# A local-attention transformer on one core: the score mask in the scores' own array tiling, norm turns on the full array, and new step orders on five engines

## The chip, the cores and the metric

One core of a Trainium2 chip. The metric is the device time of one launch in microseconds. TensorE multiplies (its records are PE, its weight loads PEld), VectorE is DVE, ScalarE is ACT, GpSimd is POOL, SyncE is SP, which here only issues DMAs.

## What is computed

A first stage (layer norm, one attention without softmax, gates) is run once for each of 16 batches of 256 tokens with 128 channels. Then six layers, each for all 16 batches, of local attention with 16 heads of 64 and windows of 32 tokens, and of a gated feed-forward net. The change is in the attention:

```python
q = l2norm(q) * qs;  k = l2norm(k) * ksc            # norms over each head's 64 channels
q = q*cos*scale + rotate_half(q)*sin*scale           # k with 1/scale
bk2, bv2 = look(bk), look(bv)                        # the window before and this one: 64 keys
mask = (it < jb) | (it > jb + w) | (jb == -1)
sim = jnp.where(mask, -finfo.max, einsum('bhwie,bhwje->bhwij', bq, bk2) * 8.0)
out = einsum('bhwij,bhwje->bhwie', softmax(sim, -1), bv2)
```

`it` is the place of the query, `jb` of the key (-1 ahead of the first window), `w` is 32. All of it is float32.

## The kernel before

Channels lie on the partitions and tokens in the free dimension. One *period* of the main part does one batch's share of everything, and 96 batches (6 layers x 16) pass through it in three stages. `walk(order, step)` goes through an engine's order once per period; a step is done for batch g of that period, for g + 1 if its kind is in `AHEAD`, for g - 1 if it is in `BEHIND`. The orders are strings written out by hand at the top (`PE_ORDER`, `DVE_ORDER`, `ACT_ORDER`, `POOL_ORDER`, `SP_ORDER`). Engines are tied only by semaphores: `x.wait_ge(sem, at(g, n, k))` waits for k of the n events that batch g brings.

The steps of TensorE, in the trace by their lines:
- PA, PB 0 to 3 (L1234, ahead): projections of k (0, 1) and q (2, 3), halves a and b of each head.
- V0 to V3 (L1279, ahead): values. 
- NK, NQ (L1245, ahead): sums of squares of k and q per head, with `head_ones` loaded in four column tiles of 32; TK, TQ (L1253): their transposes.
- TU (L1260, ahead): turns `rk_bf`, the inverse norms of k in three bf16 parts, 3 x 16 = 48 columns, so that heads lie on partitions. UC copies it to `rkt`. KN0, KN1 (L1269, ahead) spread it over the channels with `head_sel_bf`, 48 rows deep.
- S00, S01, S10, S11: scores of token tile 0 and 1, in two halves of 64 matmuls each. Each matmul is 64 rows by 32 columns of the array (`qt` loaded, `kt` moving, 64 columns): 2 banks (e) by 4 windows (w) is 8 places. Ahead of S00 and S10 the mask is put into the two banks (L1289): identity times `mask_bf`, 128x128, 512 columns.
- T (L1308): transposes of the probabilities; PV (L1326): probabilities times values, 64x64 pieces.
- WO (L1336), CEN, VAR (L1350, L1354), UP (L1365), DN (L1372), BI (L1345), all behind: output projection, layer norm, feed-forward.

DVE: XS copies the shifted input, RA and RB (L993) multiply the projections with the rotary tables, M (L1026, L1031) takes row maxima, XA and XB (L1059 to L1064) add the residual behind WO, AR (L1045) inverts the sums, KM (L1009) scales k, TC (L1038), UC and VC (L1015) copy out of PSUM. ACT: Q squares (L730), E exponentials (L774), OC (L763) and VC (L736) copies, RTK and RTQ norms, G gelu. POOL: AD0 to AD3 (L617) add the two products into `ks` (0, 1) and `qs` (2, 3), AN (L601) divides the probabilities, RK (L587 to L595) splits the inverse norms into bf16 parts, TB0 to TB3 (b = 15 of a layer only) make the next layer's tables.

SP issues, in its order, only once the wait in front of each is over:
- MQ and MK (L476): `move`, 8 DMAs of 128 KB each, from `qs` to `qt` and from `ks` to `kt`. MQ waits for AD3 (`rot_ready`), MK for KM1 (`kn_ready`); both are of the batch ahead, and S00 of the next period waits for them.
- MV (L487): `move_v`, 16 DMAs from `vs` to `v2`, after the period's last PV and the VC copies.
- LS, LK, LV, LL: loads of the next layer's weights. LK and LV only for b = 15 of their batch, LL for b = 4, layers 0 to 4. LV (L454, 512 KB) first waits for the last V of its batch, as `wv` has one buffer. LL (L458 to L466) is five loads, 1 MB.

PSUM: the steps PA, PB, TU, KN, V, T, DN (and PAD, a place left empty) take three banks in turn, `ring_ps`; a step waits until the reader of the step three places before is done (`bank_free`).

Of the kernel before, what the change touches and what calls it, by code (L numbers as in the profile page):

```python
# [8 lines left out]
BF16 = mybir.dt.bfloat16  # L9
# [4 lines left out]
P = 128  # L14
BATCH, TOKENS, DIM = 16, 256, 128
DEPTH, HEADS, DIM_HEAD, WINDOW = 6, 16, 64, 32
# [3 lines left out]
PAIRS = HEADS // 2  # L20
TILES = TOKENS // P
WINDOWS = TOKENS // WINDOW
WPT = P // WINDOW
KEYS = 2 * WINDOW
# [3 lines left out]
HALF = DIM_HEAD // 2  # L28
QUADS = HEADS // 4
COUPLES = QUADS // 2  # L30
QK_BANKS = 4 * COUPLES
MOVES = 8
V_MOVES = 16
# [5 lines left out]
MASKED = -1e30  # L39
# [11 lines left out]
PA0 PB0 PA1 S00 S01 PB1 BI WO PA2 NK CEN PB2 VAR PA3 PB3 TK UP0 UP1 S10 S11 V0 UP2 T00 TU NQ KN0 PAD V1 PV00 KN1  # L51
TQ T01 V2 DN T10 PV01 V3 T11 PV10 PV11
"""
DVE_ORDER = """
XS RA0 RB0 RA1 M0 RB1 BI XA XB AR00 RA2 RB2 CK XG RB3 RA3 H0 M1 AR01 H1 TC00 UC H2 KM0 CQ VC1 KM1 AR10 TC01 X
AR11 TC10 VC3 TC11
"""
ACT_ORDER = """
QA0 QB0 QA1 E00 QB1 E01 E02 SQ QA2 LN E03 QB2 RTK LG G0 QB3 QA3 G1 VC0 G2 LE E10 E11 E12 E13 VC2 OC00 OC01 OC10
RTQ OC11  # L60
"""
POOL_ORDER = """
AD0 AD1 AD2 AN00 AD3 RK TB0 AN01 TB1 AN10 TB2 AN11 TB3
"""
SP_ORDER = """
LS LK MQ MK LV LL MV
# [52 lines left out]
def build(nc, t):  # L119

    with ExitStack() as ctx:
        def sb(name, shape, dt=F32):
            return ctx.enter_context(nc.sbuf_tensor(name, shape, dt))
# [5 lines left out]
        score_ps = [ctx.enter_context(nc.psum_tensor(f"score_ps{e}", [P, 512], F32)) for e in range(2)]  # L129
# [9 lines left out]
        mask_bf = sb("mask_bf", [P, TILES, PAIRS, KEYS], BF16)  # L139
        head_ones = sb("head_ones", [P, WINDOW])  # L140
        head_sel_bf = sb("head_sel_bf", [3 * HEADS, QUADS, P], BF16)
# [32 lines left out]
        rk_bf = sb("rk_bf", [P, TILES, 3, HEADS], BF16)  # L174
        rkt = sb("rkt", [3 * HEADS, TOKENS], BF16)
# [105 lines left out]
        mask = carve(P, TILES, KEYS)  # L281
        head_sel = carve(3 * HEADS, QUADS, P)
# [58 lines left out]

        def moved(g, n=0, moves=MOVES):

            return (g + n) * (16 * moves)
# [57 lines left out]
        def bank_of(s):  # L402

            return ring_ps[RING.index(s) % BANKS]
# [14 lines left out]
        def _(sp):  # L419
# [20 lines left out]
            for dst, src in ((mask[:, :, :], t["mask"]), (head_ones[:, :], t["head_ones"]),  # L440
                             (head_sel[:, :, :], t["head_sel"]), (rotary[:, :, :], t["rotary"])):
                sp.dma_start(dst, src).then_inc(consts_landed, 16)
# [90 lines left out]
        def _(pool):  # L533
# [4 lines left out]
            pool.memset(ones_bf[:, :], 1.0)  # L538
            pool.memset(kt[:, :, 0:WINDOW], 0.0).then_inc(memset_done, 1)
# [7 lines left out]
            pool.wait_ge(consts_landed, 16 * 4)  # L547
# [5 lines left out]
            for i in range(TILES):  # L553
                for j in range(PAIRS):
                    last = pool.tensor_copy(mask_bf[:, i, j, :], mask[:, i, :])
# [255 lines left out]
        def _(dve):  # L811
# [161 lines left out]
            def step(s, g, b, parity, layer):  # L973
# [24 lines left out]
                if kind == "UC":  # L998
                    dve.wait_ge(rk_turned, at(g, 1, 1))
                    dve.wait_ge(kn_made, at(g, COUPLES))  # L1000
                    turn = bank_of(("TU",))[0:3 * HEADS, 0:TOKENS // 2].bitcast(BF16)
                    V.tensor_copy(rkt[:, :], turn).then_inc(rkt_ready, 1)
                if kind == "KM":
                    c = s[1]
# [88 lines left out]
        def _(pe):  # L1093
# [129 lines left out]
            def step(s, g, b, parity, layer):  # L1223
# [31 lines left out]
                if kind == "TU":  # L1255
                    pe.wait_ge(rk_parts, at(g, 4, 4))
                    bank_free(g, s)
                    turn = bank_of(s)[0:3 * HEADS, 0:TOKENS // 2].bitcast(BF16)
                    for i in range(TILES):
                        last = pe.transpose(turn[:, P * i:P * (i + 1)],  # L1260
                                            rk_bf[:, i, :, :].rearrange("p a h -> p (a h)"), ident_bf[:, :])
                    last.then_inc(rk_turned, 1)
# [18 lines left out]
                if kind == "S":  # L1281

                    i, half = s[1], s[2]
                    if half == 0:
                        pe.wait_ge(exp_ready, at(g, TILES * PARTS, PARTS * i))
                        for e in range(2):
                            if e == 1 and i == 0:
                                pe.wait_ge(q_moved, moved(g, 1))
                            mm(score_ps[e][:, :], ident_bf[:, :], mask_bf[:, i, :, :].rearrange("p j c -> p (j c)"),  # L1289
                               start=True, stop=False, skip_group_check=True)  # L1290
# [98 lines left out]
def shape_constants():  # L1389
# [12 lines left out]
    query = np.arange(P)[:, None] % WINDOW  # L1402
    key = np.arange(KEYS)[None, :]
    hidden = (key > query + WINDOW) | (query > key)
    mask = np.zeros((P, TILES, KEYS), np.float32)
    for i in range(TILES):
        no_window = (i == 0) & (np.arange(P)[:, None] < WINDOW) & (key < WINDOW)
        mask[:, i] = np.where(hidden | no_window, MASKED, 0.0)
    head_ones = np.zeros((P, WINDOW), np.float32)
    head_sel = np.zeros((HEADS, QUADS, P), np.float32)  # L1410
    for r in range(4):
        head_ones[HALF * r:HALF * (r + 1), r] = 1.0
        for u in range(QUADS):
            head_sel[4 * u + r, u, HALF * r:HALF * (r + 1)] = 1.0
    return {"ident": np.eye(P, dtype=np.float32), "mask": mask, "head_ones": head_ones,
            "head_sel": np.concatenate([head_sel] * 3), "rotary": rotary,
# [40 lines left out]
```

## Time and profile before

| what | us |
|---|---|
| median of 3 runs (lowest, highest) | 3449.61 (3441.67, 3456.11) |
| the profiled execution, its own time | 3448.65 |
| its span, first to last instruction | 3446.9 |
| busy: PE, ACT, DVE, POOL | 3333.7, 2701.8, 2439.3, 1445.0 |
| mean granted clock of TensorE | 0.991 |

The first scores start at 197.7 us; what is before them is the first stage. In the rows, start and duration stand ahead of the engine; starts count from the span's start. Every float32 matmul leaves two records, as it goes through the array in parts. The end of a matmul in the rows is modelled, so the time that a group takes is best read from its start to the next group's start.

### The profile page before, as it was taken

The page shows a single profiled execution, that of the slowest core. Times are in us where ns is not written, and L with a number is a line of the kernel's source. Part 1 is how long each engine was busy: PE and PEld are TensorE (multiplying, and loading weights), DVE is VectorE, ACT ScalarE, POOL GpSimd, SP SyncE. Part 2 cuts the span into 40 slices and gives each one's busy share as a digit, 9 for nine tenths or more (in the row PEclk, how much of TensorE's full clock was granted, in tenths as well). Part 3 has the DMA queues.
Part 4 walks back from the last instruction along what each step waited for, and adds up shares of the span by engine and source line. Part 5 has one row for each costly group of instructions (what it writes and reads, how often), then busy time and mean ns, then how long its engine had stood idle before and what let it go on. Part 6 is the DMA issues. An engine that isn't in the chain of part 4 may idle for free.

```text
span 3446.9 us, 152524 instructions
## 1 busy us (share of the span) xinstructions
PE 3333.7 (97%) x63228; PEld 2469.4 (72%) x63228; DVE 2439.3 (71%) x5141; ACT 2701.8 (78%) x9033; POOL 1445.0 (42%) x1276
## 2 busy tenths in 40 slices
PE   7789999999999999999999999999999999999997
PEld 4457777777777777777777777777777777777775
DVE  5667777777777777777777777777777767777773
ACT  5667887878787787878788787877878787887875
POOL 2244443444444354444444443453434444443441
PEclk9999999999999999999999999999999999999998
DMA  2056655665655666565565655565565656556563
GB/s 73 1 109 132 131 123 126 134 136 115 147 118 125 129 137 132 128 131 123 120 148 117 139 128 128 122 138 127 121 141 120 132 127 133 122 121 136 114 135 75
DMA packets 361274, 421.43 MB, mean 122 GB/s; under 512 B 52291, under 2 KB 265814, under 8 KB 359814
## 3 DMA queue, kind: packets, MB, share of 16 engines
q1 hardware_dynamic: 360582, 411.67, 55.2%
q8 instruction: 499, 8.18, 1.0%
q14 instruction: 193, 1.58, 0.1%
HBM read 19.30 MB, written 2.10 MB: 6 GB/s over the span
## 4 chain that ended last, share of the span: by engine, by line
PE 70%; POOL 18%; issue 4%; DVE 2%; ACT 1%; DMA 0%; SPq 0%; POOLq 0%; DVEq 0%
PE ring_ps L1234 16%; POOL qs L617 13%; PE out_ps L1326 12%; PE out_ps L1336 10%; PE ring_ps L1279 8%; PE small_ps L1245 6%; PE score_ps L1297 4%; PE ring_ps L1308 4%; PE ring_ps L1372 4%; POOL probs L601 3%; DVE prod L993 2%; PE ring_ps L1269 2%; PE out_ps L1350 2%; PE score_ps L1289 1%; PE small_ps L1253 1%
## 5 line engine op out<-in xcount | busy, mean ns | idle before, releaser
L774 ACT ACTIVATE probs<-score_ps,neg_max,rq 128x64 f32<-128x64 f32 x3072 | 1194.7, 420 | 95.7 <-DVE neg_max L1031 94.5
L993 DVE TENSOR_TENSOR prod<-ring_ps,tables 128x512 f32<-128x512 f32 x1536 | 956.9, 680 | 285.6 <-PE ring_ps L1234 257.8
L617 POOL TENSOR_TENSOR ks<-prod 128x1024 f32<-128x1024 f32 x192 | 452.7, 2358 | 852.5 <-DVE prod L993 852.4
L1234 PE MATMUL ring_ps<-xs,wqk 128*128 128x256 f32 x3072 | 768.9, 388 | 15.5 <-issue 10.6
L774 ACT ACTIVATION_READ_ACCUMULATOR probs<-score_ps,neg_max,rq 128x1 f32 x3072 | 677.1, 220 | 0.0
L730 ACT ACTIVATE square<-ring_ps,biases 128x512 f32<-128x512 f32 x768 | 516.9, 687 | 197.2 <-DVE prod L993 196.0
L1234 PEld LDWEIGHTS ring_ps<-xs,wqk 128*128 128x128 f32 x3072 | 571.1, 191 | 104.3 <-issue 17.6
L601 POOL TENSOR_TENSOR probs<-probs,inv_sums 128x512 f32<-128x512 f32 x384 | 401.1, 1045 | 576.0 <-DVE inv_sums L1045 576.0
L617 POOL TENSOR_TENSOR qs<-prod 128x1024 f32<-128x1024 f32 x192 | 453.4, 2361 | 395.4 <-DVE prod L993 395.4
L1326 PEld LDWEIGHTS out_ps<-pt,v 64*64 64x64 f32 x24576 | 397.0, 135 | 113.5 <-issue 111.6
L763 ACT ACTIVATE att_t<-out_ps 128x512 f32<-128x512 f32 x384 | 217.0, 591 | 297.3 <-PE out_ps L1326 297.2
L1326 PE MATMUL out_ps<-pt,v 64*64 64x32 f32 x24576 | 430.2, 221 | 6.9 <-issue 4.8
L1279 PE MATMUL ring_ps<-wv,xs 128*128 128x512 f32 x768 | 425.5, 636 | 0.7 <-ACT vs L736 0.7
L1336 PE MATMUL out_ps<-att_t,wo 128*128 128x256 f32 x1536 | 351.6, 382 | 2.2 <-ACT att_t L763 1.2
L1297 PEld LDWEIGHTS score_ps<-kt,qt 64*32 64x32 f32 x24576 | 264.4, 105 | 90.6 <-issue 82.2
L1336 PEld LDWEIGHTS out_ps<-att_t,wo 128*128 128x128 f32 x1536 | 293.2, 191 | 43.4 <-issue 1.8
L1038 DVE COPY pt<-ring_ps 128x512 f32<-128x512 f32 x384 | 259.3, 675 | 82.0 <-PE out_ps L1326 78.5
L1297 PE MATMUL score_ps<-kt,qt 64*32 64x64 f32 x24576 | 297.6, 225 | 6.4 <-issue 4.0
L1009 DVE TENSOR_TENSOR ks<-ks,ring_ps 128x512 f32<-128x512 f32 x384 | 246.6, 683 | 64.3 <-PE ring_ps L1269 63.9
L1365 PE MATMUL out_ps<-xg,w 128*128 128x256 f32 (+1 forms) x1152 | 282.3, 381 | 3.5 <-DVE xg L1069 3.2
L1026 DVE TENSOR_REDUCE row_max<-score_ps 128x8 f32<-128x512 f32 x384 | 246.2, 683 | 22.8 <-PE score_ps L1297 18.9
L1365 PEld LDWEIGHTS out_ps<-xg,w 128*128 128x128 f32 (+1 forms) x1152 | 198.1, 179 | 80.7 <-DVE hidden L1076 30.9
(182 smaller groups left out, 3835.6 us busy)
## 6 DMA issues: line engine op xcount, KB each, us to landing
v<-vs SPq DMA_DIRECT2D x1344, 128.0 KB
qt<-qs SPq DMA_DIRECT2D x768, 128.0 KB
kt<-ks SPq DMA_DIRECT2D x768, 128.0 KB
v<-vs SPq DMA_DIRECT2D x192, 64.0 KB
wqk<-in_L_ffn_Wqkv SPq DMA_DIRECT2D x6, 1024.0 KB, 5.1
wv<-in_L_ffn_Wqkv SPq DMA_DIRECT2D x6, 512.0 KB, 5.8
wo<-in_L_ffn_Wo SPq DMA_DIRECT2D x6, 512.0 KB
out_dram<-ks SPq DMA_DIRECT2D x16, 128.0 KB, 1.9
```

Source lines behind the costliest of these rows:

```text
L601: pool.tensor_tensor(probs[i][:, part, :, :].rearrange("p j e k -> p (j e) k"), probs[i][:, part, :, :].rearrange("p j e k -> p (j e) k"), ...
L617: pool.tensor_tensor(dst, prod_a[p % 2], prod_b[p % 2], ALU.add).then_inc(rot_ready, 1)
L730: nc.scalar.activation(square[p % COUPLES][a][:, :], bank_of(("PB" if a else "PA", p))[:, :], ACT.Square, bias=zero_col[:, :]).then_inc(sq ...
L774: last = nc.scalar.activation(probs[i][:, j, e, :], score_ps[e][:, KEYS * j:KEYS * (j + 1)], ACT.Exp, bias=neg_max[:, h:h + 1], scale=rq[p ...
L993: last = V.tensor_tensor((prod_b if a else prod_a)[p % 2][:, f, :] .rearrange("p (u c) -> p u c", u=2), bank[:, :].rearrange("p (u c) -> p ...
L1038: V.tensor_copy(pt[:, 4 * c:4 * c + 4, :], bank_of(("T", i, c))[:, :].rearrange("p (j c) -> p j c", c=P)).then_inc(t_copied, 1)
L1234: last = mm(bank_of(s)[:, TOKENS * f:TOKENS * (f + 1)], wqk[:, n, 2 * c + f, a, :], xs[:, WINDOW:PADDED], start=True, stop=True)
L1279: mm(bank_of(s)[:, :], xs[:, WINDOW + P * i:WINDOW + P * (i + 1)], heads[:, :, e, :], start=True, stop=True).then_inc(v_made, 1)
L1297: last = mm(score_ps[e][WINDOW * w:WINDOW * (w + 1), KEYS * j:KEYS * (j + 1)], qt[64 * e:64 * e + 64, j, q0:q0 + WINDOW], kt[64 * e:64 * e ...
L1326: last = mm(out_ps[j % 2][side:side + 64, q0:q0 + WINDOW], v2[64 * e:64 * e + 64, WPT * i + w, DIM_HEAD * j:DIM_HEAD * (j + 1)], pt[64 * e ...
L1336: last = mm(out_ps[0][:, 0:TOKENS], wo[layer % 2][:, j, :], att_t[:, j, :], start=(j == 0), stop=(j == PAIRS - 1))
L1365: last = mm(out_ps[c % 2][0:size, TOKENS * n:TOKENS * (n + 1)], w1[layer % 2][:, col:col + size], xg[:, :], start=True, stop=True)
```

## The change

1. The mask. Before: per token tile two matmuls of 128x128 with 512 columns. After: eight of 64x32 with 512 columns, one for each of the eight places that the scores use; `mask_sel_bf` (identity of 32, and a row that switches the first window's extra mask on) is loaded and the 64-row `mask_bf` moves. q's moves are waited for ahead of the last of the eight; it was ahead of the second of two.
2. Norm turns on the full array. `rk_bf` gets 8 parts instead of 3 (five stay zero), so TU is 128x128 instead of 128x48 and KN 128x128 instead of 48x128; UC copies 128 rows.
3. The orders of all five engines. Among other things: S00 and S01 come right behind PA0 (before: behind PA0, PB0 and PA1); TU comes ahead of T01 and behind V1; KN0 and KN1 stand together behind PV00; POOL does AN00 ahead of AD1, and RK and AN01 ahead of AD3; TB0 to TB3 stand at the end; ACT's VC2 comes behind OC10; on SP, LV and LL stand ahead of MK, which was ahead of both.

```diff
 PE_ORDER = """
-PA0 PB0 PA1 S00 S01 PB1 BI WO PA2 NK CEN PB2 VAR PA3 PB3 TK UP0 UP1 S10 S11 V0 UP2 T00 TU NQ KN0 PAD V1 PV00 KN1
-TQ T01 V2 DN T10 PV01 V3 T11 PV10 PV11
+PA0 S00 S01 BI PB0 PB1 PA1 WO PA2 PB2 NK CEN PA3 TK VAR S10 S11 PB3 UP0 T00 UP1 UP2 V1 TU T01 PAD NQ PV00 KN0
+KN1 DN PV01 V0 V3 T10 TQ V2 T11 PV10 PV11
 """
 DVE_ORDER = """
-XS RA0 RB0 RA1 M0 RB1 BI XA XB AR00 RA2 RB2 CK XG RB3 RA3 H0 M1 AR01 H1 TC00 UC H2 KM0 CQ VC1 KM1 AR10 TC01 X
-AR11 TC10 VC3 TC11
+XS RA0 BI M0 RB0 RA1 RB1 XA XB AR00 RB2 CK RA2 RA3 XG AR01 RB3 H0 TC00 M1 H1 H2 VC1 TC01 UC KM0 KM1 AR10 CQ X
+AR11 VC3 TC10 TC11
 """
 ACT_ORDER = """
-QA0 QB0 QA1 E00 QB1 E01 E02 SQ QA2 LN E03 QB2 RTK LG G0 QB3 QA3 G1 VC0 G2 LE E10 E11 E12 E13 VC2 OC00 OC01 OC10
-RTQ OC11
+QA0 E00 QB0 E01 QB1 QA1 E02 E03 SQ QB2 QA2 LN RTK LG G0 QA3 QB3 G1 G2 LE E10 E11 E12 E13 VC0 OC00 OC01 OC10 VC2
+OC11 RTQ
 """
 POOL_ORDER = """
-AD0 AD1 AD2 AN00 AD3 RK TB0 AN01 TB1 AN10 TB2 AN11 TB3
+AD0 AN00 AD1 AD2 RK AN01 AD3 AN10 AN11 TB0 TB1 TB2 TB3
 """
 SP_ORDER = """
-LS LK MQ MK LV LL MV
+LS LK MQ LV LL MK MV
 """
...
-        rk_bf = sb("rk_bf", [P, TILES, 3, HEADS], BF16)
-        rkt = sb("rkt", [3 * HEADS, TOKENS], BF16)
+        rk_bf = sb("rk_bf", [P, TILES, RK_PARTS, HEADS], BF16)
+        rkt = sb("rkt", [P, TOKENS], BF16)
...
             pool.memset(ones_bf[:, :], 1.0)
+            pool.memset(rk_bf[:, :, :, :], 0.0)
...
-            for i in range(TILES):
-                for j in range(PAIRS):
-                    last = pool.tensor_copy(mask_bf[:, i, j, :], mask[:, i, :])
+            pool.tensor_copy(mask_sel_bf[:, :, :], mask_sel[:, :, :])
+            for j in range(PAIRS):
+                last = pool.tensor_copy(mask_bf[:, j, :], mask[:, :])
...
-                    turn = bank_of(s)[0:3 * HEADS, 0:TOKENS // 2].bitcast(BF16)
+                    turn = bank_of(s)[:, 0:TOKENS // 2].bitcast(BF16)
...
-                        for e in range(2):
-                            if e == 1 and i == 0:
-                                pe.wait_ge(q_moved, moved(g, 1))
-                            mm(score_ps[e][:, :], ident_bf[:, :], mask_bf[:, i, :, :].rearrange("p j c -> p (j c)"),
-                               start=True, stop=False, skip_group_check=True)
+                        for w in range(WPT):
+                            for e in range(2):
+                                if (w, e) == (WPT - 1, 1) and i == 0:
+                                    pe.wait_ge(q_moved, moved(g, 1))
+                                mm(score_ps[e][WINDOW * w:WINDOW * (w + 1), :],
+                                   mask_sel_bf[64 * e:64 * e + 64, int((i, w) == (0, 0)), :],
+                                   mask_bf[64 * e:64 * e + 64, :, :].rearrange("p j c -> p (j c)"),
+                                   start=True, stop=False, skip_group_check=True)
                     if i == 0 and half == 0:
                         pe.wait_ge(k_moved, moved(g, 1))
```

## Rows read from the trace of the kernel before

**Rows 1.** Stretch view, first to last output projection: length, busy times, granted clock, DMA share, GB/s

```profile
236.40:3416.60 3180.20, 3140.70 (x61776) 2343.76 (x61775) 2287.16 (x4629) 2554.66 (x8533) 1380.22 (x1171) 1.00 0.59 128
```

**Rows 2.** Timeline of TensorE, one period: start us, duration us, engine, line, operation, out<-in

```profile
1708.01 0.59 PE L1289 MATMUL score_ps<-mask_bf,ident_bf 128*128 128x512 bf16 x2
1708.53 1.64 PE L1297 MATMUL score_ps<-kt,qt 64*32 64x64 f32 x128
1710.10 1.13 PE L1234 MATMUL ring_ps<-xs,wqk 128*128 128x256 f32 x4
1711.07 3.62 PE L1336 MATMUL out_ps<-att_t,wo 128*128 128x256 f32 x16
1714.52 1.03 PE L1234 MATMUL ring_ps<-xs,wqk 128*128 128x256 f32 x4
...
1725.74 0.60 PE L1308 MATMUL ring_ps<-ident,probs 128*128 128x128 f32 x4
1726.40 0.29 PE L1260 MATMUL ring_ps<-ident_bf,rk_bf 128*48 128x128 bf16 x2
1726.62 1.07 PE L1245 MATMUL small_ps<-square,head_ones 128*32 128x256 f32 x16
1727.62 0.39 PE L1269 MATMUL ring_ps<-rkt,head_sel_bf 48*128 48x256 bf16 x2
1727.94 1.12 PE L1279 MATMUL ring_ps<-wv,xs 128*128 128x512 f32 x2
1729.00 1.14 PE L1326 MATMUL out_ps<-pt,v 64*64 64x32 f32 x64
1730.07 0.39 PE L1269 MATMUL ring_ps<-rkt,head_sel_bf 48*128 48x256 bf16 x2
1730.39 0.44 PE L1253 MATMUL small_ps<-ident,norm 128*128 128x128 f32 x2
...
1741.64 1.75 PE L1297 MATMUL score_ps<-kt,qt 64*32 64x64 f32 x128
```

**Rows 3.** Timelines of DVE (first row) and POOL in the same period

```profile
1715.95 0.19 DVE L1045 RECIPROCAL inv_sums<-sums 128x8 f32<-128x8 f32 x1
...
1722.80 2.36 POOL L617 TENSOR_TENSOR qs<-prod 128x1024 f32<-128x1024 f32 x1
1726.30 1.04 POOL L601 TENSOR_TENSOR probs<-probs,inv_sums 128x512 f32<-128x512 f32 x1
```

**Rows 4.** Timeline of SP's queue: issues of q's and k's moves, two periods

```profile
385.09 6.54 SPq L476 DMA_DIRECT2D qt<-qs  x8
...
1725.25 5.33 SPq L476 DMA_DIRECT2D qt<-qs  x8
1731.87 5.50 SPq L476 DMA_DIRECT2D kt<-ks  x8
```

**Rows 5.** Stretch view around these moves, columns as in rows 1

```profile
391.74:392.90 1.16, 1.16 (x7) 1.01 (x7) 0.54 (x1) 1.16 (x8) 1.04 (x1) 1.00 0.98 195
...
1733.00:1738.90 5.90, 5.90 (x206) 4.83 (x206) 3.15 (x7) 2.94 (x10) 1.06 (x2) 1.00 0.88 183
1738.90:1739.70 0.80, 0.80 (x6) 0.70 (x5) 0.11 (x1) 0.77 (x4) 0.00 (x0) 1.00 0.00 0
```

**Rows 6.** Timeline of SP's queue where a layer's weights are loaded

```profile
364.38 0.59 SPq L458 DMA_DIRECT2D wo<-in_L_ffn_Wo  x1
...
368.55 0.61 SPq L487 DMA_DIRECT2D v<-vs  x1
...
1235.19 0.59 SPq L454 DMA_DIRECT2D wv<-in_L_ffn_Wqkv  x1
```

**Rows 7.** Stretch view around a stall of TensorE, columns as in rows 1

```profile
765.04:766.73 1.69, 0.00 (x1) 0.00 (x0) 0.00 (x0) 0.00 (x0) 0.00 (x0) 1.00 0.05 10
766.73:770.60 3.87, 3.87 (x12) 3.12 (x12) 1.29 (x2) 1.96 (x5) 0.00 (x0) 0.56 0.35 77
```

## What I expect, and why

> **What bounds the kernel now.** I read four views in this order. First the busy time of the whole repeating part [rows 1]: from the first output projection to the last, 3180.2 us for 95 periods, 33.48 us each, and TensorE is busy for 3140.7 of them. So TensorE sets the time, and the question is what fills it. Second its timeline in one period [rows 2]. It repeats after 33.11 us (scores at 1708.53 and 1741.64) and runs without a hole. A step of four full-array records takes 0.86 us (WO: 16 in 3.45). Where the array's tiling changes there is more: PB1, right behind the scores, takes 0.97; V1, between the 48-row KN0 and the 64x64 PV00, takes 1.06. So a group pays 0.10 when it follows a change of tiling and 0.10 when one follows it. Third POOL and DVE around the q and k rotations [rows 3], and last the SP queue's moves and the DMA engines' share [rows 4, 5], because the new order puts the scores much nearer to the moves that feed them. In what follows times are counted from the start of the first score matmul of a period, "score 0".
>
> **Full-array norm turns.** T00 to KN1 take 4.65 us now (1725.74 to 1730.39) [rows 2]: T00 0.66, TU 0.22, NQ 1.00, KN0 0.32, V1 1.06, PV00 1.07, KN1 0.32. T00 carries 0.12 in which TU waits for POOL's rk_bf (RK ends as AN starts, 1726.30 [rows 3]). With TU and KN full and the new order, the same work is T00 0.43, TU 0.11, V1 0.86 with 0.10 before NQ, NQ 1.00, PV00 1.07, KN0 0.32 (first after a change), KN1 0.21, together 4.10. Saving 0.55 per period. The 128 rows instead of 48 cost nothing, since time goes by columns: KN still has 256. RK moves ahead of AN01 and AD3 on POOL, so TU no longer waits.
>
> **The mask.** Now two bf16 matmuls of 512 columns per token tile, 0.52 us with 0.10 for the change before the scores [rows 2]: 0.42, or 0.21 each. After: eight of 64x32, each on its own piece of the array, in the scores' own tiling. Bounds: all eight together, 0.21; one after another, 8 x 0.21 = 1.7. Nearest row: NQ, 16 records of 256 columns and two passes in four column tiles, takes 1.00 us, from 1726.62 to 1727.62 [rows 2], where one after another would be 16 x 0.216 = 3.45. The four tiles overlap almost fully. The scores say the same for the rows: 128 records of 64 columns take 1.57, or 12 ns each, where one alone would be 54 (0.216 x 64/256). I take 0.25 and keep both ends. Saving 0.17 twice, 0.35 per period. The change of tiling itself isn't saved, it now lies before the mask.
>
> The Trainium skill (TensorE: Matmul & The Clock Gate, Part 3) gives 10.6 times for 16 tiles of 512 columns, a little worse than I take; an estimate by it is 8 x 0.21 / (8 x 0.66) = 0.32 per mask, 13 us more over the kernel.
>
> TensorE's own work falls by 0.9, from 33.1 to 32.2 us per period. If it stayed the bound, 95 x 0.9 = 86 us would go.
>
> **The new order, against what the moves need.** Score 0 of a batch needs all 16 moves of its q and k (MQ, MK; 1 MB each), which DVE's KM1 and POOL's AD3 of the period before release. Now PA0, PB0 and PA1 stand ahead of score 0; after, only PA0. MK is issued at 1731.87 and score 0 comes at 1741.64, 9.77 us later [rows 2, 4]. Its packets end at 1738.9, 7.0 after the issue [rows 5]; that is a good case. In another period MQ is issued at 385.09 [rows 4] and the engines are still at share 0.98 from 391.74 to 392.90 [rows 5], 7.8 after it, so a set takes 7.0 to some 8.5, and score 0 has had 1.3 to 2.8 us of room.
>
> After, on POOL: WO ends at 7.7 (scores 1.57, PB0 0.97, PB1 and PA1 1.72, WO 3.45). XA, XB and AR00 follow it as now, until 1.6 later (1714.52 to 1716.14) [rows 2, 3]: 9.3. AN00 now comes ahead of AD1: 10.4. AD1 and AD2 at 2.36 each: 15.2. RK 1.2: 16.4. AN01 1.04: 17.4. AD3: 19.8 [rows 3]. Nothing of this leaves POOL idle. RB3, which AD3 also needs, is done by 16.9. MQ is issued from 19.9 (now 16.7), its eight issues take 5.2, and KM1 is done at 24.8; so MK starts at 25.1, right behind MQ instead of 1.3 us after its last issue, and lands 7.0 to 8.7 later, plus up to 0.5 since MQ's packets are still in the engines. I take 8.0: 33.1, with 0.1 for the semaphore 33.2. TensorE would be there at 32.2. So it waits about 1 us at every score 0, and the period is 33.2 (bounds 32.2 and 34.0), hardly below today's 33.11.
>
> Part of today's mean over 33.11 (0.37) lies in short stalls of TensorE before the scores, such as the 1.69 us from 765.04 [rows 7]; behind a wait for DMA most of it is covered. I take 33.25 as the mean: 95 x (33.25 - 33.48) = -22 us.
>
> The Trainium skill (DMA: Bandwidth & Descriptors, Specifications) lets packets of 512 B and more run at up to 435 GB/s. An estimate by it has the moves limited by their issues alone, and the wait gone. The rows show 183 GB/s at share 0.88 with 1 KB packets [rows 5], so the trace disagrees.
>
> **What is queued ahead of MK on SP.** The new SP order has LV and LL before MK; both are there five times (layers 0 to 4). LL issues five loads and holds SP for 4.2 us (364.38 to 368.55) [rows 6]; now only the v moves stand behind it. MK starts at 29.3 instead of 25.1 and the wait for it grows by 4.1. LV first waits for V2. PV10 and PV11 (2.1), T11 (0.5), PA0 (0.96) and the mask (0.25) lie between V2's end and the next score 0, so V2 ends near 28.3; LV's issue is 0.6 [rows 6]: MK starts at 29.0, and half a megabyte of weights shares the engines with it (2.9 us at 180 GB/s; I take half): 5.5. Together 5 x 9.6 = 48 us. Bounds: 3 and 7 for each, 30 to 70.
>
> With waits of 5 to 6 us the clock comes in. After 1.69 us of idle the granted clock was 0.56 for 3.87 us [rows 7], most of it at the lower of its two levels, 1.2 GHz: 3.87 x 0.44 = 1.7 us lost. I price each of the ten long waits with that: 17 us (0 to 35).
>
> LL's data is wanted much later, and TB0 to TB3 now stand behind AN11: DVE's first rotation of a layer comes 1.4 us later, under LV's wait. VC2 now comes behind OC10 and delays the v moves by 1.3 us, with 7 to spare before PV00. The smaller mask set-up lies under the first stage. All at nothing; without LV's wait TB would cost 5 x 1.4 = 7 us.
>
> **Sum.** 3448.65 (the profiled execution's time; span 3446.9, median of the runs 3449.61) - 22 + 48 + 17 = 3492; I say 3490.
>
> **Rivals.**
> - *The moves land in time*: 12.3 us after MQ's issue (5.2 + 7.1, as in the good case). The wait vanishes and the mean is 32.2 + 0.37 = 32.6: -84, + 65 at the layers' ends: 3430. For it: the good case is real. Against: MQ's packets in front. 0.18.
> - *Moves in time and the layers' ends nearly free* (SP gets through LL and LV under other work): 3365. Against: there is nothing between MK and score 0 that could wait. 0.07.
> - *The transfers of a pair queue up fully* (slower side, one mechanism): both sets at 7 us of packets, 1.2 + 14, give a period of 34.1; from 13.6 us for the pair on the kernel is slower even without the layers' ends. 95 x 0.6 + 65: 3570. 0.12.
> - *The eight mask matmuls don't overlap* (the change doesn't do what it says): 1.7 instead of 0.42. The first lies partly in the wait, the second adds 1.3 per period: 3610. NQ's row speaks against it. 0.04.
> - *Forecast*, 3455 to 3535: 0.55. 0.04 for what lies between it and the first rival.
>
> The range is 3400 to 3560, leaving out most of the second, third and fourth rival. A measurement of this kernel can tell 0.5% from no change: faster than 3432, 0.22 (second rival, most of the first); between, 0.18; slower than 3467, 0.60.
>
> **What would show it.** In the profile after: T00 to KN1 near 4.1 us; each mask group about 0.25 ahead of the scores; TensorE waiting for DMA kt at nearly every score 0, about 1 us, and ten times 5 us or more, with the clock down behind them; SP's MK issue 5.2 us after MQ's, and 9 us after it ten times. If score 0 waits for nothing in ordinary periods, the first rival holds. If the period is under 32.5 my walk of POOL or the transfer time is wrong.

## The result and the profile after

After takes 3656.44 us in the median (3642.6 to 3671.03), before 3451.07 beside it: a ratio of 1.0599 [1.0552, 1.0646], 205 us slower. The forecast was 3490 in a range of 3400 to 3560. The sign was right, the size was not. The profiled execution of after took 3655.21 us, with a span of 3653.4 and a mean granted clock of 0.963; before it was 3446.9 and 0.991. Times here and below are medians of fast executions; the one slow execution, 3744.09 us at a granted clock of 0.844, of the second kernel of experiment 3, is left out.

The busy time of the repeating part comes first, first to last output projection (length, busy times, granted clock, DMA share, GB/s), after:

```profile
241.08:3623.27 3382.19, 3127.98 (x62907) 2382.20 (x62906) 2322.01 (x4629) 2530.09 (x8526) 1376.38 (x1172) 0.97 0.53 120
```

A period is now 35.60 us instead of 33.48 [rows 1]. TensorE is busy for 12.7 us less in all, although its clock is lower. It stands idle for 254 us where it was idle for 40: 215 more, less the 12.7, are the 202 us by which this part grew. The waits of TensorE (line waited for, sum, times, longest), after and then before:

```profile
PE score_ps L1304 <- DMA kt<-ks: 193.0, 81, 6.2
PE out_ps L1333 <- issue: 27.2, 16, 2.1
...
PE score_ps L1304 <- issue: 20.4, 25, 1.9
```

```profile
PE ring_ps L1234 <- issue: 10.6, 13, 1.6
...
PE score_ps L1297 <- issue: 4.0, 5, 1.7
...
PE score_ps L1297 <- DMA kt<-ks: 2.3, 3, 1.6
```

There are 96 batches, and score 0 waits for k's moves 81 times; before, 3 times. The chain that ended last says the same: SP's issues (23%) and POOL (21%) are on it nearly as much as TensorE is (29%).

```profile
PE 29%; SPq 23%; POOL 21%; issue 12%; DMA 7%; DVE 3%; ACT 0%; POOLq 0%; DVEq 0%
```

One period on TensorE's timeline, after, answers [rows 2]:

```profile
1730.59 0.41 PE L1294 MATMUL score_ps<-mask_bf,mask_sel_bf 64*32 64x512 bf16 x8
1730.82 1.40 PE L1304 MATMUL score_ps<-kt,qt 64*32 64x64 f32 x113
1733.14 0.34 PE L1304 MATMUL score_ps<-kt,qt 64*32 64x64 f32 x15 [0.93 <-issue]
1733.41 2.86 PE L1238 MATMUL ring_ps<-xs,wqk 128*128 128x256 f32 x12
1736.11 3.62 PE L1343 MATMUL out_ps<-att_t,wo 128*128 128x256 f32 x16
...
1751.01 0.27 PE L1264 MATMUL ring_ps<-ident_bf,rk_bf 128*128 128x128 bf16 x2
1751.12 0.61 PE L1315 MATMUL ring_ps<-ident,probs 128*128 128x128 f32 x4
...
1763.62 0.41 PE L1294 MATMUL score_ps<-mask_bf,mask_sel_bf 64*32 64x512 bf16 x8
1767.71 1.69 PE L1304 MATMUL score_ps<-kt,qt 64*32 64x64 f32 x128 [3.67 <-DMA kt<-ks]
1769.33 4.39 PE L1238 MATMUL ring_ps<-xs,wqk 128*128 128x256 f32 x12
```

TensorE's own work from score 0 to the end of the next mask is 1763.85 - 1730.82 - 0.93 = 32.1 us. The mask takes 0.23, TU 0.11 (1751.01 to 1751.12). Score 0 then waits until 1767.71, so this period is 36.89. And the twelve matmuls behind the wait take 4.39 instead of 2.86. The moves of the same two periods on SP's queue, against [rows 4]:

```profile
1716.42 5.91 SPq L479 DMA_DIRECT2D qt<-qs  x8
1722.45 6.40 SPq L479 DMA_DIRECT2D kt<-ks  x8
1730.88 10.76 SPq L490 DMA_DIRECT2D v<-vs  x16
1751.55 7.72 SPq L479 DMA_DIRECT2D qt<-qs  x8
1759.38 6.45 SPq L479 DMA_DIRECT2D kt<-ks  x8
```

MQ is issued 20.73 after score 0 (I had 19.9), its eight issues take 7.72 (I had 5.2), and score 0 comes 8.33 behind MK (I had 8.1). The stretches around that wait, columns as in the first row:

```profile
1763.98:1767.71 3.73, 0.06 (x9) 0.00 (x1) 1.04 (x2) 1.48 (x4) 0.00 (x0) 1.00 0.62 135
1767.71:1769.30 1.59, 1.59 (x128) 1.45 (x128) 0.00 (x0) 0.00 (x0) 0.00 (x0) 0.93 0.87 193
1769.33:1771.30 1.97, 1.97 (x7) 1.61 (x6) 1.47 (x3) 0.33 (x2) 0.00 (x0) 0.50 0.89 205
1771.30:1773.56 2.26, 2.26 (x9) 1.87 (x8) 1.29 (x2) 2.12 (x10) 0.75 (x1) 0.74 0.48 111
```

After 3.7 us with almost nothing on TensorE, the granted clock is 0.93 over the scores, and 0.50, the lower level of 1.2 GHz, for the first 2 us of the full-array work behind them.

The shown period is one of the longer ones. Over the 95 steps from one score 0 to the next in the trace of after, the median is 35.5 us and the mean 35.7; before, 33.2 and 33.5. In the ten periods with LV or LL the mean is 38.15, in the other 85 it is 35.4 and the median 35.3. In the median of these 85, MQ is issued 20.8 us after score 0, its issues take 6.0, MK starts 27.1 after score 0 and score 0 comes 8.2 behind MK.

**Where 206 us of span come from.** Waits for kt: 193.0 - 2.3 = 191. Waits called "issue" at the scores, the PV products and the projections: 20.4 + 27.2 + 8.0 against 4.0 + 4.8 + 10.6, 36. Slower matmuls in two groups whose work did not change, from the groups by line (busy time, mean ns), after and before:

```profile
L1238 PE MATMUL ring_ps<-xs,wqk 128*128 128x256 f32 x3072 | 829.5, 410 | 17.7 <-issue 8.0 <-ACT square L734 5.9 <-DVE xs L984 3.6
L1304 PE MATMUL score_ps<-kt,qt 64*32 64x64 f32 x24576 | 316.9, 241 | 213.6 <-DMA kt<-ks 193.0 <-issue 20.4
```

```profile
L1234 PE MATMUL ring_ps<-xs,wqk 128*128 128x256 f32 x3072 | 768.9, 388 | 15.5 <-issue 10.6 <-DVE xs L980 4.1 <-ACT square L730 0.7
L1297 PE MATMUL score_ps<-kt,qt 64*32 64x64 f32 x24576 | 297.6, 225 | 6.4 <-issue 4.0 <-DMA kt<-ks 2.3
```

That is 60.6 + 19.3 = 80. Less work: 95 x 0.9 = 86 the other way. The 86 is the forecast's saving. Sum: 191 + 36 + 80 - 86 = 221, within 15 of the 206; the ends of matmuls are modelled, so the 80 is the roughest. The slower matmuls gave back almost all of the saving, as the 12.7 us of busy time says too.

### The profile page after: what moved, and what is told of

Read it like the earlier page. It is cut to its first block, busy times and chain, and to the rows that moved or that the text cites. A ratio compares the mean times of both kernels' runs of the same rounds, so it can differ in the third digit from the quotient of the medians.

```text
span 3653.4 us, 154823 instructions
## 1 busy us (share of the span) xinstructions
PE 3318.9 (91%) x64380; PEld 2509.2 (69%) x64380; DVE 2472.5 (68%) x5141; ACT 2677.1 (73%) x9033; POOL 1437.7 (39%) x1270
## 3 DMA queue, kind: packets, MB, share of 16 engines
q8 instruction: 508, 8.32, 1.0%
## 4 chain that ended last, share of the span: by engine, by line
PE 29%; SPq 23%; POOL 21%; issue 12%; DMA 7%; DVE 3%; ACT 0%; POOLq 0%; DVEq 0%
SPq L479 23%; POOL qs L621 8%; POOL ks L621 8%; PE ring_ps L1238 8%; DMA kt<-ks 7%; PE score_ps L1304 6%; POOL probs L605 4%; PE out_ps L1343 3%; PE out_ps L1333 2%; PE ring_ps L1283 2%; PE out_ps L1372 2%; DVE prod L997 2%; PE small_ps L1249 1%; PE ring_ps L1315 1%; DVE row_max L1030 1%
## 5 line engine op out<-in xcount | busy, mean ns | idle before, releaser
L997 DVE TENSOR_TENSOR prod<-ring_ps,tables 128x512 f32<-128x512 f32 x1536 | 978.8, 685 | 433.9 <-PE ring_ps L1238 368.7
L1238 PE MATMUL ring_ps<-xs,wqk 128*128 128x256 f32 x3072 | 829.5, 410 | 17.7 <-issue 8.0
L778 ACT ACTIVATION_READ_ACCUMULATOR probs<-score_ps,neg_max,rq 128x1 f32 x3072 | 689.9, 225 | 0.0
L1238 PEld LDWEIGHTS ring_ps<-xs,wqk 128*128 128x128 f32 x3072 | 598.9, 203 | 126.4 <-issue 21.9
L734 ACT ACTIVATE square<-ring_ps,biases 128x512 f32<-128x512 f32 x768 | 506.5, 686 | 118.1 <-DVE prod L997 114.3
L1304 PE MATMUL score_ps<-kt,qt 64*32 64x64 f32 x24576 | 316.9, 241 | 213.6 <-DMA kt<-ks 193.0
L1304 PEld LDWEIGHTS score_ps<-kt,qt 64*32 64x32 f32 x24576 | 292.7, 112 | 250.2 <-DMA kt<-ks 218.5
L1333 PE MATMUL out_ps<-pt,v 64*64 64x32 f32 x24576 | 422.9, 220 | 28.5 <-issue 27.2
L767 ACT ACTIVATE att_t<-out_ps 128x512 f32<-128x512 f32 x384 | 226.6, 639 | 303.0 <-PE out_ps L1333 303.0
L1283 PE MATMUL ring_ps<-wv,xs 128*128 128x512 f32 x768 | 387.5, 606 | 1.7 <-DVE ks L1013 1.2
L1315 PEld LDWEIGHTS ring_ps<-ident,probs 128*128 128x128 f32 x1536 | 184.2, 141 | 114.7 <-POOL probs L605 72.9
```

The costliest lines, as they stand in the source:

```text
L734: nc.scalar.activation(square[p % COUPLES][a][:, :], bank_of(("PB" if a else "PA", p))[:, :], ACT.Square, bias=zero_col[:, :]).then_inc(sq ...
L778: last = nc.scalar.activation(probs[i][:, j, e, :], score_ps[e][:, KEYS * j:KEYS * (j + 1)], ACT.Exp, bias=neg_max[:, h:h + 1], scale=rq[p ...
L997: last = V.tensor_tensor((prod_b if a else prod_a)[p % 2][:, f, :] .rearrange("p (u c) -> p u c", u=2), bank[:, :].rearrange("p (u c) -> p ...
L1238: last = mm(bank_of(s)[:, TOKENS * f:TOKENS * (f + 1)], wqk[:, n, 2 * c + f, a, :], xs[:, WINDOW:PADDED], start=True, stop=True)
L1283: mm(bank_of(s)[:, :], xs[:, WINDOW + P * i:WINDOW + P * (i + 1)], heads[:, :, e, :], start=True, stop=True).then_inc(v_made, 1)
L1304: last = mm(score_ps[e][WINDOW * w:WINDOW * (w + 1), KEYS * j:KEYS * (j + 1)], qt[64 * e:64 * e + 64, j, q0:q0 + WINDOW], kt[64 * e:64 * e ...
```

## The experiments

The theory to begin with: the loss is the wait for the moves, with what it does to the clock. The rival: TensorE would be slow in the new order even with q and k in place.

**1. The wait taken away, the moves left.** The kernel after:

```diff
-                                if (w, e) == (WPT - 1, 1) and i == 0:
-                                    pe.wait_ge(q_moved, moved(g, 1))
...
-                    if i == 0 and half == 0:
-                        pe.wait_ge(k_moved, moved(g, 1))
...
-                                          qt[64 * e:64 * e + 64, j, q0:q0 + WINDOW],
-                                          kt[64 * e:64 * e + 64, j, q0:q0 + KEYS],
+                                          still_q[64 * e:64 * e + 64, j, q0:q0 + WINDOW],
+                                          still_k[64 * e:64 * e + 64, j, q0:q0 + KEYS],
```

> The changed kernel, but its score matmuls read a part of x1_all that doesn't change in the main part instead of qt and kt, and TensorE waits for no move ahead of the scores. The moves are still issued in full. So the scores are of other data; all work and all orders stay. Theory (the wait for the moves of k, and what follows from it, is the whole loss): TensorE runs at its own 32.0 us per period plus the short stalls of before, about 32.5, so 95 x 3.1 = 295 us less than 3655: 3360 (3340 to 3390), and the granted clock is back at 0.99. Rival (the new orders or the eight small mask matmuls let the clock fall or make TensorE stall by themselves, the moves are a bystander): 3550 or more, the clock near 0.96.

Measured 3472.64. This kernel, its counterpart below, and the two others whose scores are of unchanging data were executed once each. The same edit on the kernel before:

> The same edit on the kernel before: scores of unchanging data, no wait for moves ahead of them. Theory: the moves cost the kernel before next to nothing (4 us of waits in its rows), so 3435 to 3450. Rival (the moves held it up too, by contention or by short waits that no row shows): below 3420.

Measured 3451.46, as before without it: there the moves cost nothing. After loses 184 us with its wait. But the time is neither the theory's nor the rival's: without any wait for moves the new order still takes 3473 and not 3360, more than the kernel before. What holds TensorE there is new:

```profile
PE score_ps L1303 <- issue: 81.4, 88, 2.6
PE ring_ps L1241 <- issue: 22.9, 16, 2.7
```

In 88 places TensorE stands in the middle of the scores with no semaphore, buffer or transfer to wait for, as in this period:

```profile
1714.77 0.78 PE L1303 MATMUL score_ps<-x_all 64*32 64x64 f32 x52
1716.02 1.11 PE L1303 MATMUL score_ps<-x_all 64*32 64x64 f32 x76 [0.46 <-issue]
```

It runs out of instructions. PV10, PV11, PA0, the mask and S00 and S01 now follow each other: 128 + 4 + 8 + 128 records of matmuls, each with one of a weight load, some 540 instructions in about 4.7 us. (Float32 leaves two records for each matmul of the program, so S00 is 32 matmuls and 64 records.) Before, PB0 and PA1 stood in this stretch as well, and the mask was 2 matmuls and not 8.

The trace shows the fetches themselves, as packets of 16 KB on a DMA queue of kind "instruction". In the period shown such a packet ran from 1713.57 to 1714.62, and the scores went on at 1716.02, 1.40 after its end. That is the rule: from the first scores on, 122 of the 124 stalls of TensorE without a releaser end 1.1 to 1.7 us after the end of such a packet, where instants at random would do so in 9% of cases. In after it is 52 of 52, in before 29 of 29.

**2. The moves taken away too.** All q and k moves, and POOL's waits for them, are left out of the kernel of experiment 1.

> a_still without any move of q and k: MQ and MK still wait but issue nothing, and POOL's AD0 and AD2 don't wait for them. Tells apart two reasons for the missing instructions in S00. If the fetches (16 KB each) queue behind the moves' packets on the DMA engines, they come in time now: 3400 or less. If the stretch is simply denser than the fetches can follow, nothing changes: 3460 to 3480. I lean to the first, 60 to 40.

Measured 3412.1, 60 us less than 3472.64, and between the two expectations. The wait inside the scores falls from 81.4 to 49.8 us:

```profile
PE score_ps L1301 <- issue: 49.8, 65, 2.5
```

So part of it comes only with the moves, and the larger part stays without them. This kernel also shows the saving of the change where no move disturbs it: a period less TensorE's waits is 32.3 us in the mean, against 33.2 before.

**3. Full-array work between the small matmuls.** Two kernels: that of experiment 1, and after itself, with PB0 and PB1 ahead of the scores.

```diff
-PA0 S00 S01 BI PB0 PB1 PA1 WO PA2 PB2 NK CEN PA3 TK VAR S10 S11 PB3 UP0 T00 UP1 UP2 V1 TU T01 PAD NQ PV00 KN0
+PA0 PB0 PB1 S00 S01 BI PA1 WO PA2 PB2 NK CEN PA3 TK VAR S10 S11 PB3 UP0 T00 UP1 UP2 V1 TU T01 PAD NQ PV00 KN0
```

> a_still (scores of unchanging data, no wait for moves) with one edit in TensorE's order: PA0 PB0 PB1 S00 S01 BI PA1 instead of PA0 S00 S01 BI PB0 PB1 PA1, so that 1.7 us of work with 16 instructions more stands between the dense PV10, PV11 and the dense mask and scores. Theory (in a_still TensorE runs out of instructions in S00, 1.0 us in a median period, since PV10, PV11, PA0, mask and scores are some 540 instructions in 4.7 us): S00 and S01 back to 1.5 us, period 32.2 with the short stalls, 3400 (3370 to 3420), clock 0.99. Rival (the stall in S00 has another cause that goes with the scores wherever they stand): 3460 to 3480.

Measured 3545.53, far from both. The feeding theory holds in its own row, the wait inside the scores is back to 17.6 us. But the time rises by 73 us, since the other engines kept the order made for the old place of the scores:

```profile
PE ring_ps L1241 <- ACT square L737: 70.6, 95, 2.8
...
PE out_ps L1360 <- ACT xc_sq L789: 21.3, 95, 3.0
...
PE score_ps L1303 <- issue: 17.6, 21, 1.9
```

> The changed kernel with only TensorE's order PA0 PB0 PB1 S00 S01 BI PA1. The scores come 1.7 us later behind PV11 than in the changed kernel. Theory (the short way from the moves to the scores costs the time): most of the mean wait of 2.1 us goes, and with it the clock's 0.5 us and the missing instructions; M0 and all behind it come 1.7 us later, of which I expect some 0.3 us to show: 95 x 2.2 = 210 less, 3450 (3420 to 3500). Rival (the loop only turns later by as much, since AD3 and KM1 follow the scores): 3620 or more.

Measured 3581.03, 1.0383 [1.0362, 1.0405], 75 us better than after instead of 206. The moves have their room, 33.0 us of waiting in 28 batches instead of 193.0 in 81, and the same two waits for ACT stand in their place:

```profile
PE ring_ps L1238 <- ACT square L734: 68.9, 97, 2.3
PE score_ps L1304 <- DMA kt<-ks: 33.0, 28, 4.0
...
PE score_ps L1304 <- issue: 13.1, 18, 1.4
```

**4. The wait filled, with small matmuls or with full-array ones.** If the idle time lowers the clock and that costs time, then needless work in it should help.

```diff
-                        for w in range(WPT):
+                        for n, w in [(n, w) for n in range(10 if i == 0 else 1) for w in range(WPT)]:
```

> The changed kernel with the eight mask matmuls of token tile 0 done ten times over instead of once (the same result each time, 1.9 us more of TensorE's work, most of it in what is otherwise the wait for k's moves). Theory (the wait itself is paid by the moves, and on top of it the clock falls after it and makes PB0 to PA1 slower by 0.5 us in the mean, inside the loop that leads to the next moves): the clock stays up and the time falls by some 45 us in spite of more work, 3610 (3590 to 3640). Rival (the clock costs nothing, as the wait absorbs it): 3655 to 3700.

Measured 3761.7, 1.0898 [1.0882, 1.0914]: 105 us more than after, beyond the rival's own number; what it shows is the supply of instructions, not the clock. The wait for kt falls by 141 us and the wait for instructions rises by 65, which with 95 x 2.0 = 190 us of added masks makes 114:

```profile
PE score_ps L1304 <- issue: 85.4, 65, 2.5
PE score_ps L1304 <- DMA kt<-ks: 51.6, 36, 4.7
```

The page of the profile counts the fetches: 508 packets and 8.32 MB on the queue of kind "instruction" in after, 562 and 9.21 in this kernel. The 6912 added mask matmuls with their weight loads are 13,824 instructions, so one packet of 16 KB brings 256 of them. 508 packets are 130,048 instructions, and TensorE's matmuls and weight loads are 128,760 records, so nearly every record is an instruction of its own and these packets are TensorE's.

The same place filled with nine bf16 matmuls on the full array, 1.9 us and 18 instructions:

```diff
+                        for n in range(9 if i == 0 else 0):
+                            mm(score_ps[n % 2][:, :], ident_bf[:, :], mask_bf[:, :, :].rearrange("p j c -> p (j c)"),
+                               start=True, stop=True, skip_group_check=True)
```

> The clock's question again with few instructions, since a_fill took 144 more into a stretch that is short of them. The changed kernel with nine full-array bf16 matmuls of 512 columns (18 instructions, 1.9 us) between PA0 and the mask of token tile 0, into the two score banks, which the mask then overwrites; the result stays. Theory (after a wait for k's moves the clock falls and makes the loop to the next moves longer): the wait is filled, the clock is 0.98 or more, PB0 to PA1 are back at 2.7 us, and the time falls by 40 to 60 us, 3605. Rival (the clock doesn't matter): 3655 to 3690, as some waits are shorter than the filling.

Measured 3618.1, 1.051 [1.0488, 1.0532]: 38 us less than after, with 1.9 us of useless work in every period. The wait for kt is 42.7 us in 35 batches, the mean clock 0.988 instead of 0.963, and the projections' matmuls are nearly as fast as before:

```profile
L1238 PE MATMUL ring_ps<-xs,wqk 128*128 128x256 f32 x3072 | 785.8, 394 | 17.8 <-issue 8.4 <-ACT square L734 5.6 <-DVE xs L984 3.6
```

An idle wait is thus dearer than the same wait filled. It slows the twelve matmuls behind it, DVE and POOL get their q and k later, and the next moves start later: MQ is issued 20.8 us after score 0 in the median of after's 85 ordinary periods, 19.7 here.

**5. SP's order.** After with MK ahead of LV and LL, as before.

```diff
-LS LK MQ LV LL MK MV
+LS LK MQ MK LV LL MV
```

> The changed kernel with the SP order of before: LS LK MQ MK LV LL MV. Theory: only the ten periods at the layers' loads gain, 3.8 us each above an ordinary period in the trace after, so 38 us less: 3615 (3600 to 3630). Rival (the SP order is the main cause): below 3560. Rival (loads behind MK disturb the transfers as much as ahead of it): no change, 3650.

Measured 3616.18, 1.0476 [1.0444, 1.0509]: 40 us less than after, the wait for kt 156.4 instead of 193.0. The clock hardly moves, 0.968 from 0.963. One LL in after shows the mechanism:

```profile
362.58 5.91 SPq L479 DMA_DIRECT2D qt<-qs  x8
368.54 0.60 SPq L461 DMA_DIRECT2D wo<-in_L_ffn_Wo  x1
...
371.23 6.12 SPq L479 DMA_DIRECT2D kt<-ks  x8
```

MK starts 8.65 after MQ instead of 6.0, and score 0 waits 4.25 us there. That the expected 38 us came out is in part luck: they were worked out with 3.8 us for each of the ten periods, and the trace of after has 2.7 (38.15 against 35.4), which makes 27.

**6. AD3 ahead of AN01 on POOL**, so that MQ is released 1.04 us earlier.

```diff
-AD0 AN00 AD1 AD2 RK AN01 AD3 AN10 AN11 TB0 TB1 TB2 TB3
+AD0 AN00 AD1 AD2 RK AD3 AN01 AN10 AN11 TB0 TB1 TB2 TB3
```

> The changed kernel with POOL's AD3 ahead of AN01 (AD0 AN00 AD1 AD2 RK AD3 AN01). MQ is released 1.04 us earlier and with it, since MK queues behind MQ, the pair; AN01 ends as late as AD3 did and TensorE's T01 may wait some 0.3 us. Theory (the pair of moves released by AD3 closes the loop): about 0.9 us per period, 85 us less: 3570 (3550 to 3610). Rival (KM1's release of MK closes it): no more than 20 us.

Measured 3645.93, 1.0585 [1.0559, 1.0612]: 10 us, as the rival said, and the trace has its mechanism. In after MK is issued right behind MQ's last issue, 1.2 us after KM1's end (medians). Here MQ comes 0.75 us earlier, but MK now starts 0.1 us after KM1's end, and so only 0.45 us earlier. The wait for kt falls by 74 us all the same, and T01, which needs AN01, waits for it instead:

```profile
PE score_ps L1304 <- DMA kt<-ks: 119.3, 73, 5.1
PE ring_ps L1315 <- POOL probs L605: 81.4, 97, 2.4
```

**7. The two savings in the old orders.** Before with mask and turns:

> The kernel before with the mask in the scores' tiling and the norm turns on the full array, all five orders as before. By TensorE's rows: masks 0.17 twice, turns 0.28 per period, of which about 0.17 is lost again since TU waits for RK: 0.45 x 95 = 43 us less, 3407 (3385 to 3430). The room of the moves ahead of the scores hardly shrinks. Rival (the two edits of the array's use are worth nothing once stalls follow them): 3450. Rival (they are harmful by themselves): above 3460.

Measured 3420.4, 0.9913 [0.9879, 0.9947]: 32 us, within the expected range, of the 86 that 0.9 us a period would give. The mask alone:

> The kernel before with the eight-matmul mask alone: the norm turns keep their 48 rows and every engine keeps its old order. The two parts together took 32 us off where their price on TensorE was 0.9 us a period, 86 us. My theory: the mask's part of that, 0.35 us a period or 33 us (0.17 a mask, measured 0.23 a mask in the trace of after), comes back only in part, since the fourteen instructions more for each mask stand in the same dense stretch as the scores; about 10 us is lost to TensorE waiting for instructions: 3427 (3415 to 3440), with that wait before the scores' line near 15 to 20 us in sum where before has 4. The rival: the mask gains its full price and the turns are what gave nothing, since TU waits for POOL's rk: 3417, with the wait for instructions still near 4 us.

Measured 3459.9, 1.0023 [1.0008, 1.0037]: nothing gained, a little lost, and slower than theory and rival both had it. The mask itself does what was priced, 0.23 us where there were 0.52:

```profile
1732.19 0.41 PE L1293 MATMUL score_ps<-mask_bf,mask_sel_bf 64*32 64x512 bf16 x8
1732.42 1.46 PE L1303 MATMUL score_ps<-kt,qt 64*32 64x64 f32 x128
...
1736.52 0.29 PE L1263 MATMUL ring_ps<-ident_bf,rk_bf 128*48 128x128 bf16 x2 [0.28 <-POOL rk_bf L598]
```

Its gain is lost in two places. TU reaches POOL's rk too early, and the scores and PV products wait for instructions:

```profile
PE ring_ps L1263 <- POOL rk_bf L598: 32.0, 91, 4.7
...
PE out_ps L1332 <- issue: 19.2, 18, 1.8
PE score_ps L1303 <- issue: 17.3, 17, 2.0
```

Before these were 8.3, 4.8 and 4.0: 24 + 14 + 13 = 51 us of new waits, less 6 at the projections (10.6 to 5.0). Saved were 0.30 for each mask less 0.10 for the change of tiling that now lies ahead of it, 95 x 0.4 = 38. The difference, 7, is near the 10 that were measured. The turns alone:

> The kernel before with the full-array norm turns alone; mask and all orders stay as before. Mask alone gave nothing (1.0023), mask and turns together 0.9913. If the parts add up, the turns alone are worth what lies between, 39 us: 3411. My theory: behind TU the turns take 0.2 to 0.3 us a period from TensorE (KN0, KN1 and V1 0.1 each less, some of it given back at UP0), ahead of it their gain ends in TU's wait for POOL's rk as the mask's gain did; without the mask's 28 instructions the waits for instructions stay as before: 3420 (3410 to 3430), at least as fast as both parts together. The rival, that the mask still adds something beside the turns: 3435 or more.

Measured 3426.34, 0.993 [0.9917, 0.9944]: 23 us, within the theory's range. Most of what the old orders take from the two parts comes from the turns. Whether the mask adds something beside them is not settled, since the intervals of both parts and of the turns alone overlap. With both parts the wait for rk_bf is 32.2 us, with the turns alone 7.0.

**8. Can the orders be mended?** RK ahead of AD3 in the kernel with both parts:

```diff
-AD0 AD1 AD2 AN00 AD3 RK TB0 AN01 TB1 AN10 TB2 AN11 TB3
+AD0 AD1 AD2 AN00 RK AD3 TB0 AN01 TB1 AN10 TB2 AN11 TB3
```

> b_both with POOL's RK ahead of AD3 instead of behind it. In b_both TU waits 0.45 us per period for RK, which has AD3's 2.36 us ahead of it. TensorE's own work is then 32.3 us per period: 40 us less than b_both, 3380 (3365 to 3400). q's moves start 1.2 us later and end by the time that k's start. Rival (the later q moves now delay the scores): 3420 or more.

Measured 3436.27, 0.9973 [0.9957, 0.9989], 16 us worse than with RK behind AD3 (21 by the ratios), as the rival said. The wait for rk_bf is gone, KN0 waits for DVE's copy instead, and MQ starts 1.2 us later after score 0 (medians 17.9 and 16.8):

```profile
PE ring_ps L1273 <- DVE rkt L1006: 38.3, 92, 0.4
...
PE score_ps L1304 <- DMA kt<-ks: 10.2, 11, 2.6
```

And after with the old SP order, PB0 and PB1 ahead of the scores, and DVE, ACT and POOL reordered to match:

```diff
 PE_ORDER = """
-PA0 S00 S01 BI PB0 PB1 PA1 WO PA2 PB2 NK CEN PA3 TK VAR S10 S11 PB3 UP0 T00 UP1 UP2 V1 TU T01 PAD NQ PV00 KN0
+PA0 PB0 PB1 S00 S01 BI PA1 WO PA2 PB2 NK CEN PA3 TK VAR S10 S11 PB3 UP0 T00 UP1 UP2 V1 TU T01 PAD NQ PV00 KN0
...
-XS RA0 BI M0 RB0 RA1 RB1 XA XB AR00 RB2 CK RA2 RA3 XG AR01 RB3 H0 TC00 M1 H1 H2 VC1 TC01 UC KM0 KM1 AR10 CQ X
+XS RA0 RB0 RB1 BI M0 RA1 XA XB AR00 RB2 CK RA2 RA3 XG AR01 RB3 H0 TC00 M1 H1 H2 VC1 TC01 UC KM0 KM1 AR10 CQ X
...
-QA0 E00 QB0 E01 QB1 QA1 E02 E03 SQ QB2 QA2 LN RTK LG G0 QA3 QB3 G1 G2 LE E10 E11 E12 E13 VC0 OC00 OC01 OC10 VC2
+QA0 QB0 QB1 E00 E01 QA1 E02 SQ E03 QB2 QA2 LN RTK LG G0 QA3 QB3 G1 G2 LE E10 E11 E12 E13 VC0 OC00 OC01 OC10 VC2
...
-AD0 AN00 AD1 AD2 RK AN01 AD3 AN10 AN11 TB0 TB1 TB2 TB3
+AD0 AD1 AN00 AD2 RK AN01 AD3 AN10 AN11 TB0 TB1 TB2 TB3
...
-LS LK MQ LV LL MK MV
+LS LK MQ MK LV LL MV
```

> The changed kernel with the SP order of before, and four orders mended: TensorE PA0 PB0 PB1 S00 S01 BI PA1, DVE XS RA0 RB0 RB1 BI M0 RA1, ACT QA0 QB0 QB1 E00 E01 QA1 E02 SQ E03, POOL AD0 AD1 AN00 AD2 RK AN01 AD3. From score 0 to AD3 it should be 17.8 us instead of 20.6, so the moves come in time (17.8 + 14.5 = 32.3 per period, as long as TensorE's own 32.1), and the 24 instructions of PB0 and PB1 stand where instructions were missing. If that is what cost the time: 3400 (3360 to 3440). Rival (new waits for squares and maxima as in a_gap): 3500 or more.

Measured 3515.25, 1.0223 [1.0189, 1.0258], where the rival had 3500 or more. It takes back 141 us of the loss. The largest wait that is left is that of the second mask for the exponentials that stand later in ACT's new order; it is not all, as the loss against before is 70 us and TensorE has less work here:

```profile
PE score_ps L1294 <- ACT probs L778: 57.4, 96, 0.7
```

The fastest of all kernels with the right scores is the old order with both parts, 0.9913.

## Why the prediction was right or wrong

- **TensorE's own work** (32.2 us forecast): right where the clock stays up, 32.1 in the period shown and 32.3 in the mean of experiment 2. In after the slower matmuls take it back to 33.1 in the mean, where before has 33.2. The mask was priced at 0.25 and takes 0.23; its eight matmuls overlap, so that rival is out. The estimate of 0.32 by the Trainium skill (TensorE: Matmul & The Clock Gate, Part 3), worked out from its row for another tiling, was too high. "The 128 rows cost nothing": right, TU takes 0.11.
- **Which engine is late next** (score 0 waits for DMA kt at nearly every batch): right, 81 of 96.
- **The size of that wait**: wrong, and this is the step that failed. I had MQ at 19.9, issues of 5.2, MK at 25.1 and score 0 8.1 behind it, hence 1 us of waiting and a period of 33.2. In the median of the 85 ordinary periods MQ comes at 20.8, its issues take 6.0, MK starts at 27.1 and score 0 comes 8.2 behind it: 35.3. So the landing was right, and the 2 us lie ahead of MK's start, about half in MQ's lateness and half in SP's issues. My 5.2 for the issues lay below all three of [rows 4]: 6.54, 5.33 and 5.50. MQ is late by what the walk left out, slow matmuls and stalls behind score 0: with the clock kept up (experiment 4) it comes at 19.7. In means, ordinary periods of 35.4 instead of 33.25 are 206 us over the forecast, and the periods with loads 38 under it; together 168, where the forecast missed by 166.
- **The rival that the transfers of a pair queue up fully**: its time came nearest, but by its own terms it was mis-added. 19.9 + 1.2 + 14 is 35.1 and not 34.1, which makes 3449 + 154 + 65 = 3668 and not 3570. Its mechanism is not what the trace shows: the last packet comes 14.2 us behind MQ's issue where it had 15.2, and 7.8 behind MK's (medians). In the period shown the engines were at share 0.55 while MQ was issued, and at 0.77 and 0.63 from there to score 0. The issues took long, the engines were not full. With the sum put right, it would have met the time by luck.
- **The clock only at the ten long waits** (17 us): wrong. Waits at ordinary periods drop it as well: 0.50 behind 3.7 us, and matmuls slower by about 80 us over the kernel. That it feeds back was in no term: the matmuls that it slows are those that q and k are made from. Filling the wait with full-array work made the kernel 38 us faster.
- **What is queued ahead of MK on SP** (48 us, and 17 for the clock): right in mechanism, MK starts 8.65 after MQ at an LL where I had 9.4; both terms together measured 40 instead of 65. In the trace of after the ten periods are 2.7 us longer than the others, 27 us.
- **The moves in time would give 3430, with free ends 3365**: wrong even as rivals. With no wait at all for the moves the new order takes 3473, since TensorE then lacks instructions. I saw short stalls ahead of the scores in before [rows 7] and let the wait for the moves cover them; the denser order makes them more frequent, 88 times in experiment 1, where before had 5.
- **A gain of 86 us if TensorE stayed the bound**: the work fell by that much (0.9 us a period in experiment 2), the time did not. In the old orders both parts give 32, the mask alone nothing. "RK moves ahead ... so TU no longer waits" was a condition of the gain and not an extra: where RK stays behind AD3, the mask's saving ends at TU, and where RK goes ahead, the moves are late.

**What stays open.** That TensorE lacks instructions at these stalls is shown by the packets; why a fetch comes too late is not, nor why the moves make it worse by 32 us. What stretches SP's issues from 5.3 to 6.0 us is not settled either. The clock, the stalls and the late moves feed each other in the ordinary periods, and the runs don't part them fully.

## What to carry to other kernels

When an order is made anew, price the time from the last producer to the first consumer of every transfer by its slow cases, not its best one: the pair of moves had about 2 us to spare (median from the last packet to score 0), and the reorder took more than that away. A saving on the busiest engine counts only as far as the next engine's slack. The mask's 0.4 us a period were real, and POOL's rk and the supply of instructions were the end of them. Small matmuls that fill the array well still have to be fetched, so keep full-array work between long runs of them.

## What the runs showed of the hardware

- TensorE can run out of instructions. With about 540 in 4.7 us it stood 81.4 us at the scores, 49.8 without the q and k moves, 17.6 with eight full-array records of matmuls between. Instructions come in 16 KB packets of 256, and a stall ended 1.1 to 1.7 us after the end of a packet.
- Idle time of TensorE costs twice. After 3.7 us of it, full-array matmuls ran at a granted 0.50, the level of 1.2 GHz, for 2 us; nine needless matmuls in every period made the kernel 38 us faster.
- The eight issues of a set of moves by SP took from 5.3 to 7.7 us in the rows shown; what sets the length was not found. The Trainium skill (DMA: Bandwidth & Descriptors, Specifications) gives 435 GB/s as the ceiling, and 512 B as the least transfer for the full rate. Around the wait shown the engines were at share 0.87 to 0.89 with 193 to 205 GB/s, so this trace does not come near it.
- Eight bf16 matmuls of 512 columns in 64x32 tiles took 0.23 us together. The Trainium skill (TensorE: Matmul & The Clock Gate, Part 3) has a model beside the row that the prediction used: the duration of one matmul and about 4 ns for each further tile. An estimate by it is 0.21 + 7 x 0.004 = 0.24, and the trace agrees.
